# A half group's maxima split into two parts on GpSimd before the transpose, and copied out of the bank by ScalarE

## The reference

```python
q, k, v = (qkv[0], qkv[1], qkv[2])
q = apply_rotary(q, cos, sin)
k = apply_rotary(k, cos, sin)
attn = jnp.einsum('bhqd,bhkd->bhqk', q, k) * scale
attn = jax.nn.softmax(attn, axis=-1)
out = jnp.einsum('bhqk,bhkd->bhqd', attn, v)
```

## Time and profile before

| | |
|---|---|
| median of 3 runs | 1182.59 us (1181.22 to 1183.35) |
| the profiled execution's own time | 1181.48 us |
| its span in the trace | 1179.7 us |
| TensorE matmul busy | 1083.5 us, 92% |
| TensorE weight load busy | 595.9 us, 51% |
| VectorE busy | 1016.5 us, 86% |
| ScalarE busy | 768.6 us, 65% |
| GpSimd busy | 352.6 us, 30% |
| self-attention in the span | about 101 to 787 us |
| reduces, line 810 | 1024, mean 0.680 us |
| exponentials, line 748 | 512, mean 1.027 us |
| cast, line 823 | 32, mean 0.270 us |
| subtraction, line 825 | 32, mean 0.278 us |
| TensorE's clock from 161 to 900 us | 1.0 of full speed granted |

### The profile page before, as it was taken

How to read it: one execution, slowest core, us unless ns; L and a number is a source line. 1 busy time by engine, 2 the same in 40 slices (tenths; PEclk the granted TensorE clock), 3 DMA queues, 4 the chain that set the end, 5 groups by cost and what they waited for, 6 DMA issues and landing times. The chain is left out here.

```text
span 1179.7 us, 22856 instructions
## 1 busy us (share of the span) xinstructions
PE 1083.5 (92%) x8540; PEld 595.9 (51%) x8540; DVE 1016.5 (86%) x2168; ACT 768.6 (65%) x932; POOL 352.6 (30%) x316
## 2 busy tenths in 40 slices
PE   7899999999999999999999999998984059999998
PEld 6775333333333333333333333347773048888897
DVE  8999889999999999999999999716998985766663
ACT  4551378888888888888887888863565014555653
POOL 2657812202220221122022000022100023765675
PEclk9997699999999999999999999999997559999999
DMA  7787664504422441343044100036532022554443
GB/s 240 252 267 232 148 101 98 96 18 78 75 57 39 81 77 31 65 79 70 22 84 75 21 12 17 17 103 214 178 108 95 0 72 65 152 146 122 111 112 36
DMA packets 84681, 113.95 MB, mean 97 GB/s; under 512 B 25056, under 2 KB 57568, under 8 KB 84576
## 3 DMA queue, kind: packets, MB, share of 16 engines
q1 hardware_dynamic: 66256, 69.82, 20.0%
q0 software_dynamic: 15024, 36.17, 17.2%
q10 hardware_dynamic: 3296, 6.56, 1.5%
HBM read 73.31 MB, written 38.27 MB: 95 GB/s over the span
## 5 line engine op out<-in xcount | busy, mean ns | idle before, releaser
L810 DVE TENSOR_REDUCE b_max_halves<-banks 128x1 f32<-128x512 f32 x1024 | 626.7, 680 | 14.3 <-PE banks L878 14.2
L748 ACT ACTIVATE b_probs<-banks 128x1024 f32<-128x1024 f32 x512 | 520.7, 1027 | 146.4 <-PE banks L929 146.4
L878 PE MATMUL banks<-b_k,b_q 62*128 62x512 f32 x1024 | 398.7, 470 | 6.7 <-DVE b_max_halves L810 1.8
L929 PE MATMUL banks<-b_q,b_k 64*128 64x512 f32 x1024 | 385.8, 456 | 3.8 <-DMA b_q<-b_max_rows 3.5
L900 PE MATMUL banks<-b_probs,b_v 128*17 128x256 f32 (+1 forms) x3840 | 315.5, 401 | 0.2 <-ACT b_probs L748 0.2
L929 PEld LDWEIGHTS banks<-b_q,b_k 64*128 64x128 f32 x1024 | 156.9, 186 | 224.2 <-issue 167.8
L878 PEld LDWEIGHTS banks<-b_k,b_q 62*128 62x128 f32 x1024 | 162.0, 190 | 41.6 <-DVE b_max_halves L810 39.3
L900 PEld LDWEIGHTS banks<-b_probs,b_v 128*17 128x17 f32 x3840 | 63.9, 95 | 165.6 <-issue 95.9
L551 POOL TENSOR_TENSOR b_att<-b_out,b_rec_spread 128x512 f32<-128x512 f32 x32 | 41.1, 1284 | 311.5 <-DMA b_rec_spread<-reciprocals 311.2
L483 POOL DMA_DIRECT2D b_q<-q_stacks x60 | 31.8, 533 | 227.8 <-PE banks L900 215.6
L1849 DVE TENSOR_TENSOR e_hTl<-e_hT,e_hTh 128x512 fp32r<-128x512 f32 x64 | 47.6, 745 | 48.3 <-ACT e_hT L1603 48.3
(11 more groups left out here) (259 smaller groups left out, 1477.9 us busy)
## 6 DMA issues: line engine op xcount, KB each, us to landing
e_w<-in_w SPq DMA_DIRECT2D x16, 1024.0 KB
q_stacks<-a_parts SPq DMA_DIRECT2D x32, 256.0 KB, 4.0
k_stacks<-a_parts SPq DMA_DIRECT2D x32, 256.0 KB, 4.1
b_q<-q_stacks POOLq DMA_DIRECT2D x30, 256.0 KB, 5.3
b_k<-k_stacks POOLq DMA_DIRECT2D x30, 256.0 KB, 6.4
v_tiles<-a_v ACTq DMA_DIRECT2D x8, 544.0 KB, 3.7
b_rec_spread<-reciprocals SPq DMA_DIRECT2D x128, 32.0 KB, 1.8
attended<-b_att SPq DMA_DIRECT2D x128, 32.0 KB, 2.7
```

Of the source, the lines that this page charges most:

```text
L748: nc.scalar.activation(pr[:, S % NP, u], ps[:, 2 * u:2 * u + 2, :], ACT.Exp, scale=D ** -0.5).then_inc(s_ex[u], 1)
L810: v.tensor_reduce(mxp[:, (k // NB) % 2, s, p, t, kh:kh + 1], ps[:, bank(last), :], AX.X, ALU.max)\
L878: nc.tensor.matmul(ps[:, bank(last), :], qs[g][stack, p, at:at + P], ks[g][stack, p, CH * kh:CH * kh + CH], start=True, stop=True).then_in ...
L929: return nc.tensor.matmul(ps[:, 2 * u + s, :], ks[g][stack, u, P * kt:P * kt + P], qs[g][stack, u, CH * h:CH * h + CH], start=True, stop=True)
```

## The change

The maxima are split before the turn, in SBUF, where both parts fit side by side: `b_max_parts` is 128x2x16. `parts` makes them with a cast and a subtraction. GpSimd runs it at the end of its list for each half group; for the first two half groups VectorE does. The turn then has 32 weight columns and gives 32 rows, the leading parts in rows 0 to 15 and the rest in rows 16 to 31. ScalarE copies them out of the bank with one instruction, between the two exponentials of `kt` = 5 (`turned`). The turn now waits for the parts instead of for `combine`, and it stands one half step later, after the values of the first half step of `kt` = 5. For this the places are numbered anew: 0 and 2 are the two half steps' maxima, 1 lies between. VectorE's cast and subtraction go, and so do the zeros in `b_max`. The eight transfers read the same amounts from other partitions.

```diff
-                            k = PER * (KT * hg + kt) + AHEAD + 2 * place + x
-                            if place < 2 and not (last and k >= MAXS):
+                            k = PER * (KT * hg + kt) + AHEAD + place + x
+                            if place != 1 and not (last and k >= MAXS):
                                 work.append(("max", k))
-                        if place == 2 and kt == LATE and not (last and hg == NH - 1):
+                        if place == 1 and kt == LATE + 1 and not (last and hg == NH - 1):
                             work.append(("rows", hg + 1))
...
+        def parts(e, eng, n):
+
+            eng.wait_ge(s_mx, n + 1)
+            e.tensor_copy(mp[:, 0], mx[:]).then_inc(s_lead, 1)
+            eng.wait_ge(s_lead, 2 * n + 1)
+            e.tensor_tensor(mp[:, 1], mx[:], mp[:, 0].bitcast(F32), ALU.subtract).then_inc(s_lead, 1)
...
+            def turned(m, last):
+
+                act.wait_ge(s_mm, m + 1)
+                nc.scalar.activation(mT[:], ps[0:2 * 4 * NT, bank(last), 0:P], ACT.Copy).then_inc(s_ra, 1)
...
                         for u in range(2):
+                            if u == 1:
+                                for kind, k, m in at[hg, kt, 1]:
+                                    turned(n["items"] + m, len(START) + m)
...
                         tail.scale(pool, g_, 8 * i + hg - 2, hg % 2, 4 * i + (hg - 2) // 2 + 1)
+                    if not (first and hg == 0) and not (last and hg == NH - 1):
+                        parts(g_, pool, 8 * i + hg + 1)
...
-            def rows(n, m, last):
-
-                rows_ = ps[0:4 * NT, bank(last), 0:P]
-                dve.wait_ge(s_mm, m + 1)
-                v.tensor_copy(mT[:, 0, :], rows_).then_inc(s_lead, 1)
-                dve.wait_ge(s_lead, n + 1)
-                v.tensor_tensor(mT[:, 1, :], rows_, mT[:, 0, :].bitcast(F32), ALU.subtract).then_inc(s_ra, 1)
...
             def rows(hg, n, items, m, last):
-                pe.wait_ge(s_mx, hg + 1)
+                pe.wait_ge(s_lead, 2 * hg + 2)
                 free(n, items, m)
-                nc.tensor.matmul(ps[:, bank(last), 0:P], mx[:], ident[:], is_transpose=True, start=True, stop=True)\
+                nc.tensor.matmul(ps[0:2 * 4 * NT, bank(last), 0:P], mp[:].rearrange("p r m -> p (r m)").bitcast(F32), ident[:],
+                                 is_transpose=True, start=True, stop=True)\
                     .then_inc(s_mm, 1)
```

More of the change, by code:

```diff
@@ L597, in attend @@
         mxp = sb("b_max_halves", [P, 2, 2, 2, NT, 2])
-        mx = sb("b_max", [P, P])
-        mT = sb("b_max_rows", [4 * NT, 2, P], F32R)
+        mx = sb("b_max", [P, 4 * NT])
+        mp = sb("b_max_parts", [P, 2, 4 * NT], F32R)
+        mT = sb("b_max_rows", [2 * 4 * NT, P])
         osb, rb = tail.osb, tail.rb
@@ L604, in attend @@
         s_one = [sem(f"b_minus_rows_in{g}") for g in range(NG)]
-        s_zero = sem("b_max_cleared")
         s_ld = [group0[3]] + [sem(f"b_loaded{g}") for g in range(1, NG)]
@@ L613, in attend @@
         s_ra = sem("b_max_rows_taken")
-        s_lead = sem("b_max_rows_leading")
+        s_lead = sem("b_max_parts_ready")
         s_mx = sem("b_max_ready")
@@ L677, in rows @@
                         eng.dma_start(qs[g][at:at + 1, p, CH * h:CH * h + CH].bitcast(F32),
-                                      mT[m:m + NT, r, :].bitcast(F32)).then_inc(s_row[h], 16)
+                                      mT[4 * NT * r + m:4 * NT * r + m + NT, :]).then_inc(s_row[h], 16)
+        def parts(e, eng, n):
[3 more added lines that the diff above has]
+            e.tensor_tensor(mp[:, 1], mx[:], mp[:, 0].bitcast(F32), ALU.subtract).then_inc(s_lead, 1)
         block = ctx.enter_context(nc.Block(no_gpsimd_drain=True))
@@ L735, in take @@
                 nc.scalar.activation(osb[:, x, :], ps[:, PV, :], ACT.Copy).then_inc(s_oe, 1)
+            def turned(m, last):
+                act.wait_ge(s_mm, m + 1)
+                nc.scalar.activation(mT[:], ps[0:2 * 4 * NT, bank(last), 0:P], ACT.Copy).then_inc(s_ra, 1)
             def body(i, first, last):
+                at, items = plan(last)
+                n = before(i, first)
                 for hg in range(NH):
@@ L750, in _ @@
             end_leading(act)
+            turned(NB, NB)
             act.wait_ge(s_ra, 1)
@@ L815, in combine @@
                 dve.wait_ge(s_mr, NB * n + NB)
-                v.tensor_tensor(mx[:, 0:4 * NT].rearrange("p (s q t) -> p s q t", s=2, q=2), mxp[:, h, :, :, :, 0],
+                v.tensor_tensor(mx[:].rearrange("p (s q t) -> p s q t", s=2, q=2), mxp[:, h, :, :, :, 0],
                                 mxp[:, h, :, :, :, 1], ALU.max).then_inc(s_mx, 1)
-            def rows(n, m, last):
-                rows_ = ps[0:4 * NT, bank(last), 0:P]
-                dve.wait_ge(s_mm, m + 1)
-                v.tensor_copy(mT[:, 0, :], rows_).then_inc(s_lead, 1)
-                dve.wait_ge(s_lead, n + 1)
-                v.tensor_tensor(mT[:, 1, :], rows_, mT[:, 0, :].bitcast(F32), ALU.subtract).then_inc(s_ra, 1)
             v.memset(ps[:, PV, :], 0.0)
-            v.memset(mx[:], 0.0).then_inc(s_zero, 1)
             for m, (kind, k) in enumerate(START):
@@ L831, in _ @@
                     reduce(k, m, m)
-                else:
-                    rows(0, m, m)
                 if k == NB - 1:
-                    dve.wait_ge(s_zero, 1)
                     combine(0, 0)
+                    parts(v, dve, 0)
             def body(i, first, last):
@@ L846, in body @@
                                     reduce(k, n["items"] + m, len(START) + m)
-                                else:
-                                    rows(8 * i + hg + 1, n["items"] + m, len(START) + m)
                             if place == 0 and kt == LATE and not (last and hg == NH - 1):
                                 combine(8 * i + hg + 1, (hg + 1) % 2)
-                            if place == 1 and kt == KT - 1 and not (first and hg == 0):
+                                if first and hg == 0:
+                                    parts(v, dve, 1)
+                            if place == 2 and kt == KT - 1 and not (first and hg == 0):
                                 tail.invert(dve, v, 8 * i + hg - 1, (hg - 1) % 2)
@@ L951, in body @@
                             for x in range(2):
-                                ring(hg, kt, u, x)
+                                ring(hg, kt, 2 * u, x)
                             scores(g, h, S, u, 1).then_inc(s_st[u], 1)
@@ L955, in body @@
                                 earlier(S, 2, 1)
+                                ring(hg, kt, 1, 0)
                             else:
                                 earlier(S, 1, 0)
-                        ring(hg, kt, 2, 0)
             bodies(pe, body)
```

## The result

| | before | after |
|---|---|---|
| median | 1181.90 us (1181.02 to 1183.35, 4 runs) | 1194.51 us (1192.61 to 1194.80, 4 runs) |
| profiled execution | 1181.48 us, span 1179.7 | 1192.61 us, span 1190.8 |

The ratio is 1.0095 [1.0083, 1.0107]: slower by 0.95%. The forecast was 1194.1 us.

The account below looks back on a forecast made before the run. TensorE was taken to pace the kernel, with VectorE held to it. New waits 8.1, starts without slack 3.2 and +0.2 before the body gave +11.5 us: 1193.0 profiled, 1194.1 as median, range 1182 to 1205.

Parts of the forecast that it names:

- VectorE's 0.51 us are worth nothing: Self-attention half groups: removing VectorE's cast and subtraction, 0.51 us each half group, gains nothing because TensorE sets the pace.
- the other case: Rival in self-attention: VectorE was the bound, each half group gets 0.51 us shorter, 15.8 us in all, 1167; chance 0.09.
- GpSimd's parts are covered: Before the turn: GpSimd's cast and subtraction take 0.5 us within 1.75 us of cover, cost 0.
- The turn still costs TensorE about the same: At the turn: 32 weight columns instead of 128 cost TensorE 0.2 to 0.26 us, against 0.26 before.
- ScalarE's copy: After the turn: copy starts 0.49 us later, lasts 0.275, first issue at 0.79, quicker than VectorE by 0.41 us.
- The new wait of 0.30 us: Next half group's start: rows ready 6.92 us after the turn, TensorE at 6.62; 27 x 0.30 = 8.1 us.
- before the first start: Before the body: VectorE makes the first half group's parts while ScalarE's copy is quicker, +0.2 us (0 to 0.4).
- the term of the starts without slack: Half group starts already waiting for rows: four lose the whole 0.81 us each, 3.2 us together.

Follow-up runs that it names:

- the four transfers: Changed kernel with the rows of maxima moved by four transfers instead of eight: 1178.16 us, 0.9949 of the kernel before; run again, 1177.60 us, 0.9964.
- loaded twice: Changed kernel with four transfers instead of eight and four unused additions per half group on VectorE: 1186.04 us, 1.0030 of the kernel before.

## Why the prediction was right

**VectorE's 0.51 us are worth nothing: right.** The kernel with the turn put back has them removed and takes as long as before; 0.40 us put in again cost nothing in either version. The mark named for the other case, reduces at 0.596 us from one to the next, did not come: 0.611.

**GpSimd's parts are covered: right.** Cast and subtraction take 0.20 and 0.22, 0.49 us from the cast's start to the subtraction's end (0.5 was taken), and are over at 419.50, 1.19 us before the turn. The cover was so thick only because of the later turn: one half step earlier the subtraction is 0.09 us late.

**The turn still costs TensorE about the same: right.** Its next scores start 0.22 us later (0.26 before), and the reduce that is waited for there is still waited for.

**ScalarE's copy: right to 0.03 us.** Start 0.50 after the turn (0.49 predicted), length 0.25 (0.275), first issue at 0.78 (0.79).

**The new wait of 0.30 us: right.** 6.92 us from the turn to the next start, as predicted, where TensorE would have been ready after 6.62; half groups have a median of 20.61 us (20.6), against 20.31 before. The two single experiments put bounds on it from both sides: without the later turn it disappears, without the quicker copy it is about 0.4 longer, and half the transfers remove it.

**The terms beside it: mis-sized in both directions, and the sum came out by luck.** From the start times of TensorE's first scores in each half group:

| term | predicted | measured |
|---|---|---|
| before the first start | +0.2 | +1.13 (130.76 to 131.89) |
| from the first start to the last | +11.3 | +8.83 (637.62 to 646.46) |
| from the last start to the end | 0 | +1.17 (411.30 to 412.48) |
| together | +11.5 | +11.1 |

Of the 31 half groups that another one follows, 24 lengthen by some 0.3 us (0.27 to 0.34) as forecast. Three, the first of each later batch, lengthen by only 0.03 (20.91 to 20.95 before, 20.94 to 20.97 after). There the wait takes the place of another: before, TensorE stood in the batch's first half step until a reduce was done, and that step took 1.87 us; in the change it starts 0.33 us late and takes 1.53.

The step that failed is the term of the starts without slack, 4 x 0.81 = 3.2. The sum took four starts with waits of 0.47 us on average for the ones without slack, and counted the two with long waits (3.18 and 1.35 us) among the 27 with 0.51 of slack. A wait of 0.47 us, hardly over the usual 0.42, did not mean that the start had no slack. The half groups that end at the four lengthen by 0.11, 0.27, 0.03 and 0.62 us, 1.0 together. At the first of them the rows were late for a reason that does not move with the turn: SyncE was still issuing the stores of an output, so the first issue came 1.91 us after the turn (211.48) and not 1.20.

```profile
211.38 1.97 SPq L558 DMA_DIRECT2D attended<-b_att  x4
213.39 5.02 SPq L677 DMA_DIRECT2D b_q<-b_max_rows  x8
```

In the change the issue there comes 0.78 us after the turn, as elsewhere. At the other three the eight issues took 5.27 to 5.37 us before instead of 5.03; in the change only the last of them does (5.37), and there the idle time is 1.07 us. Of the two with long waits, the half group that ends at the last start lengthens by 0.78, nearly the whole 0.81. The one that ends at the second start gets shorter, 26.19 to 26.00 us: its way from the first issue to the scores takes 9.31 us before and 8.29 after, instead of 6.13, and why is open.

Of the +1.17 at the end, 1.08 lie between the last half group's first scores and its last (14.94 to 16.02 us), and there the clock was lower. A stretch behind the last start, first before, then in the change, with the columns of the earlier trace rows; the last three numbers are the granted clock, the DMA share and GB/s:

```profile
768.40:772.40 4.00, 3.87 (x34) 1.31 (x34) 0.00 (x0) 3.48 (x5) 0.38 (x1) 1.00 0.12 33
779.30:782.60 3.30, 3.30 (x24) 0.88 (x20) 0.00 (x0) 2.32 (x3) 0.59 (x1) 0.50 0.14 40
```

In the change TensorE had stood idle for 1.66 us before this start; then the granted clock was 0.50 (1.2 GHz of 2.4), and two half steps took 1.71 and 1.67 us instead of 0.99. The kernel with only the turn moved shows the same after 1.86 us. The change with VectorE loaded does not: 1.67 us idle, a clock of 1.00, and 14.92 us. So the longer wait for the rows did not bring this every time, and the sum has no term for it. The whole stretch from the last start to the end stands at 413.04, 411.87, 411.38 and 412.57 us in four others of these kernels; the 413.04 of the four transfers has its excess behind self-attention.

The first term was too small. Counted from the first reduce, so that its own place (101.95 and 101.75 us) does not count, the way to the first scores goes from 28.80 to 30.14 us, +1.34. With the cast at the start gone it is 29.09, +0.29, and that is about what was forecast; the last section says what the rest is. So +2.5 too much in the body stands against 0.9 and 1.2 too little around it.

## What to carry to other kernels

Before work is moved off an engine that looks full, compare the start to start time of its instructions where something feeds it with the same where nothing but it limits: 0.610 against 0.596 us said here that VectorE, busy for 98.95%, was not the bound. When a step is moved later, measure the slack of everything that starts from it (here 0.51 us) and subtract the whole shift, net of what got quicker on the way. If the slack is spent in transfers that are issued one behind the other, fewer and larger ones can buy more of it than work taken off an engine: four instead of eight took 2.3 us off the issue, on a path that lacked 0.3, where the quicker copy had taken off 0.4 and the work taken off VectorE nothing.

## What the runs showed of the hardware

The prediction had +0.2 us for making the first half group's parts on VectorE. The way from the first reduce to the first scores grew by 1.34. VectorE in the change, and what GpSimd did at the same time, from 117 us on:

```profile
121.00 0.18 DVE L836 TENSOR_TENSOR b_max<-b_max_halves 128x16 f32<-128x16 f32 x1
121.22 1.17 DVE L683 CAST b_max_parts<-b_max 128x16 fp32r<-128x16 f32 x1
122.42 0.17 DVE L685 TENSOR_TENSOR b_max_parts<-b_max,b_max_parts 128x16 fp32r<-128x16 f32 x1
123.80 0.69 DVE L830 TENSOR_REDUCE b_max_halves<-banks 128x1 f32<-128x512 f32 x1 [1.21 <-PE banks L887]
```

```profile
118.69 3.65 POOL L471 MEMSET b_q<- 32x2048 f32 x2
122.41 3.65 POOL L471 MEMSET b_k<- 32x2048 f32 x2
```

A cast of 16 columns takes 1.17 us and ends at 122.39, just behind GpSimd's second memset of the first pair (118.69 + 3.65 = 122.34). Its neighbours of the same size take 0.17 and 0.18 while such a memset runs. The kernel without the cast shows the other half:

```profile
121.72 0.18 DVE L835 TENSOR_TENSOR b_max<-b_max_halves 128x16 f32<-128x16 f32 x1
121.81 0.17 DVE L844 TENSOR_TENSOR b_max_parts<-b_max_halves 128x16 fp32r<-128x16 f32 x1
122.08 0.18 DVE L848 TENSOR_TENSOR b_max_parts<-b_max,b_max_parts 128x16 fp32r<-128x16 f32 x1
123.47 3.08 DVE L829 TENSOR_REDUCE b_max_halves<-banks 128x1 f32<-128x512 f32 x5 [1.21 <-PE banks L891]
```

```profile
119.38 3.65 POOL L471 MEMSET b_q<- 32x2048 f32 x2
123.08 3.65 POOL L471 MEMSET b_k<- 32x2048 f32 x2
```

The maximum that takes the cast's place, two operands in SBUF, runs in 0.17 us in the middle of a memset, and from the combine to the next reduce there are 123.47 - 121.72 = 1.75 us instead of 123.80 - 121.00 = 2.80. The Trainium skill (SBUF — State Buffer, Who interferes with whom) says this: VectorE and GpSimd share a port pair that whoever comes first holds for its whole instruction; copies and casts within SBUF can go through it, while a two-operand instruction is held up only by a GpSimd instruction that reads SBUF. Both runs agree, 1.17 us against 0.17. Eight traces have the cast in this place: it takes from 0.32 us (four transfers, VectorE loaded) to 1.40 (loaded twice), and in each it ends 0.03 us after a memset does, so its length goes by what is left of that memset when it begins. The same cast takes 0.17 us on VectorE in the body of the change (at 146.74), with no memset beside it, and 0.20 on GpSimd for the later half groups.
